# Clears and first loads of the next phase within the last batch, and a split of keys moved within its loop

## Time and profile before

| | us |
|---|---|
| three runs | 2462.93, 2463.0, 2460.99; median 2462.93 |
| profiled execution, own time | 2466.63 |
| its span, first to last instruction | 2464.5 |
| mean granted TensorE clock | 0.943 of full |
| busy: PE 2156.1, DVE 1533.1, ACT 1363.7, POOL 697.1 | shares 87%, 62%, 55%, 28% |

### The profile page before, as it was taken

One profiled execution on the slowest core, in us unless ns is written; L12 is line 12 of the kernel. 1 busy time (PEld: TensorE's weight loads), 2 busy tenths in 40 slices (PEclk: granted clock), 3 DMA queues, 4 the chain that ended last, 5 costly groups with the idle time before them and its releaser, 6 DMA issues. The chain is left out here.

```text
span 2464.5 us, 49127 instructions
## 1 busy us (share of the span) xinstructions
PE 2156.1 (87%) x15930; PEld 1268.1 (51%) x15930; DVE 1533.1 (62%) x3120; ACT 1363.7 (55%) x2226; POOL 697.1 (28%) x577
## 2 busy tenths in 40 slices
PE   3763899999999999999938999999998399999587
PEld 2331677777777777777724444444443144444132
DVE  2663788888888888888743434434432566666354
ACT  1441566666666666666724554454553166666464
POOL 1443544444444444444401122222123000000000
PEclk9885999999999999999968999999998699999799
DMA  5333111111111111111011122122211222222221
GB/s 179 104 114 91 33 36 33 33 33 33 33 33 33 33 33 33 33 32 32 20 31 60 65 94 67 56 90 68 94 69 34 73 91 90 89 89 69 90 90 35
DMA packets 156366, 151.01 MB, mean 61 GB/s; under 512 B 83656, under 2 KB 113874, under 8 KB 155026
## 3 DMA queue, kind: packets, MB, share of 16 engines
q1 hardware_dynamic: 150930, 148.11, 20.5%
q10 hardware_dynamic: 5376, 2.12, 0.3%
HBM read 96.08 MB, written 54.12 MB: 61 GB/s over the span
## 5 line engine op out<-in xcount | busy, mean ns | idle before, releaser
L1141 ACT ACTIVATE prob<-prob,neg_max_h 128x640 f32<-128x640 f32 x512 | 424.3, 829 | 329.4 <-DVE neg_max_h L1039 329.0
L1039 DVE CUSTOM_DVE_ANT_0 prob<-pair,pair_mask 128x640 f32<-128x640 f32 x512 | 418.9, 818 | 153.2 <-PE pair L956 153.0
L1102 POOL TENSOR_TENSOR a_full<-rot_c,rot_s 128x512 f32<-128x512 f32 x128 | 163.0, 1273 | 501.9 <-DVE rot_s L1026 501.9
L1622 PE MATMUL pair<-hid,down_w 128*128 128x512 f32 x640 | 295.6, 607 | 3.3 <-ACT hid L1548 3.3
L1046 DVE TENSOR_TENSOR prob<-prob 128x128 f32<-128x128 f32 x512 | 273.6, 534 | 0.5 <-ACT prob L1141 0.5
L1548 ACT ACTIVATE hid<-pair,up_b 128x512 f32<-128x512 f32 x320 | 198.6, 692 | 106.2 <-PE pair L1602 105.9
L912 PE MATMUL turn<-ident,prob 128*128 128x128 f32 x1024 | 250.4, 275 | 0.1
L912 PE MATMUL outsum<-ident,prob 128*128 128x128 f32 x1024 | 249.7, 275 | 0.5 <-ACT prob_t L1149 0.5
L1920 ACT ACTIVATE prob_h<-pair 128x512 f32<-128x512 f32 (+1 forms) x352 | 186.7, 561 | 102.7 <-PE pair L1820 98.5
L1875 DVE TENSOR_REDUCE row_max<-pair 128x1 f32<-128x384 f32 (+3 forms) x352 | 199.4, 634 | 32.6 <-PE pair L1795 31.9
L1622 PEld LDWEIGHTS pair<-hid,down_w 128*128 128x128 f32 x640 | 121.9, 193 | 150.9 <-issue 130.7
(11 more groups left out here) (270 smaller groups left out, 4324.1 us busy)
## 6 DMA issues: line engine op xcount, KB each, us to landing
o_d<-out_sb SPq DMA_DIRECT2D x64, 256.0 KB, 2.0
w_all<-w_d SPq DMA_DIRECT2D x8, 2048.0 KB, 10.8
vx_d<-vx SPq DMA_DIRECT2D x8, 1024.0 KB, 4.9
val_h<-vx_d SPq DMA_DIRECT2D x32, 256.0 KB
qs_d<-part_q SPq DMA_DIRECT2D x48, 128.0 KB
ks_d<-part_k SPq DMA_DIRECT2D x48, 128.0 KB
num<-o_d SPq DMA_DIRECT2D x24, 256.0 KB
den<-o_d SPq DMA_DIRECT2D x24, 256.0 KB
```

Of the source, the lines that this page charges most:

```text
L1039: nc.vector.tensor_tensor_reduce(prob[s % 4][:, :], pair[:, cols], pair_mask[:, cols], -1.0, 3.0e38, ALU.add, ALU.min, neg_max[par][:, s:s ...
L1102: nc.gpsimd.tensor_tensor(a_full[h % 2][:, :], rot_c[h % 2][:, :], rot_s[h % 2][:, :], ALU.add).then_inc(a_steps.sem, 1)
L1141: nc.scalar.activation(prob[s % 4][:, :], prob[s % 4][:, :], ACT.Exp, bias=neg_max[par][:, s:s + 1], scale=-1.0).then_inc(exp_done.sem, 1)
L1622: mm = nc.tensor.matmul(out_ap, down_w[:, EXPERTS[i], c, :], hid[i % 2][:, c, :], start=(c == 0 and i != 1), stop=(c == HC - 1 and i != 0))
```

## The change

1. `meet` is new: drain, count, wait, for some engines alone. PE, DVE, POOL and ACT meet between projection and layer-0 heads (`proj_met`, 4), PE, DVE and ACT between feed-forward and layer-1 heads (`ffn_met`, 3). SP is in neither. The three other barriers stay.
2. The clears of the layer-0 heads move into the projection's last batch: on DVE behind the rest of qu, on POOL between the last weight split and the last split of qv. Allocation is reordered so that the cleared tiles lie over nothing that is still in use, and three waits for stores are added within group 0 of the heads.
3. SP's first loads of the heads (`sp_first`) move into the last batch's stage 2, behind the store of the edge and ahead of the three stacks.
4. In every turn of the projection the keys' split stands right behind the edge product; keys are stored first of the three stacks.
5. In the feed-forward's `last`, DVE clears the layer-1 buffers behind the centre and writes the one-hot rows ahead of the queries' split; SP loads the first two groups ahead of the last stores; groups 2 and 3 are loaded by `h1_sp` behind the wait for all stores. ACT gets two waits for stores at its start.

```diff
+        def meet(eng, met, engines):
+            eng.drain().then_inc(met, 1)
+            eng.wait_ge(met, engines)
...
+        def clear_heads_v(v):
+            v.wait_ge(weight_parts.sem, weight_parts.at(2 * (B + NSH)))
+            for i in range(2):
+                nc.vector.memset(qs[i][:, :, :], 0.0).then_inc(heads_init, 1)
+                nc.vector.memset(ks[i][:, :, :], 0.0).then_inc(heads_init, 1)
+                nc.vector.memset(a_hi[i][:, :, S:AW], 0.0).then_inc(heads_init, 1)
+                nc.vector.memset(a_lo[i][:, :, S:AW], 0.0).then_inc(heads_init, 1)
+        def clear_heads_pool(g):
+            g.wait_ge(weight_parts.sem, weight_parts.at(2 * (B + NSH)))
...
             def stage2(b):
+                if isinstance(b, int) and b == B - 1:
+                    sp.wait_ge(v_stored.sem, v_stored.at(32 * (B - 1)))
...
                 sp.dma_start(one(ed_d, b), edge[:, :]).then_inc(edge_stored.sem, 16)
+                if isinstance(b, int) and b == B - 1:
+                    for stored in (qu_stored, qv_stored, k_stored):
+                        sp.wait_ge(stored.sem, stored.at(stack_dmas * (B - 1)))
+                    h0[5](sp)
+                sp.wait_ge(p2_dve.sem, p2_dve.at("k_3", b))
+                store_stack(sp, ks_d, b, part_k, k_stored.sem)
                 sp.wait_ge(p2_dve.sem, p2_dve.at("qu_3", b))
...
                 if project_of is not None:
                     edge_products(project_of)
+                    v.wait_ge(k_stored.sem, k_stored.at(stack_dmas * project_of))
+                    split(v, ve, kt, part_k, rest_k, p2_dve, "k", project_of)
...
                     rest_parts(qu, part_q, rest_q, "qu", project_of)
-                    v.wait_ge(k_stored.sem, k_stored.at(stack_dmas * project_of))
-                    split(v, ve, kt, part_k, rest_k, p2_dve, "k", project_of)
+                    if isinstance(project_of, int) and project_of == B - 1:
+                        clear_heads_v(v)
...
+            with g.Fori(0, B - 1) as b:
+                split_weights(b, b + NSH)
+                split_qv(b)
+            split_weights(B - 1, B - 1 + NSH)
+            clear_heads_pool(g)
+            split_qv(B - 1)
...
             def last(b):
                 store_x2(b)
                 load_mod1(b)
+                sp.wait_ge(v1_stored.sem, v1_stored.at(16 * b))
+                sp.wait_ge(q1_stored.sem, q1_stored.at(stack_dmas * b))
+                sp.wait_ge(k1_stored.sem, k1_stored.at(stack_dmas * b))
+                sp.wait_ge(h1_init, H1_INIT)
+                h1_load(sp, 0, 0)
+                h1_load(sp, 1, 1)
                 stores(b)
...
             def last(b):
                 ln1.center(v, "d", b, x2, f3_pe, f3_dve)
+                clear_h1(range(H1_BUFS))
                 adaln1(b)
                 bound_q(b)
                 bound_k(b)
+                one_hot_h1(v)
                 split_q(b)
...
             proj_sp(sp)
+            h0[0](sp)
             barrier(sp, 1)
-            h0[0](sp)
+            ffn_sp(sp)
+            h1_sp(sp)
             barrier(sp, 2)
...
             proj_v(v)
+            meet(v, proj_met, 4)
+            h0[2](v)
             barrier(v, 1)
-            h0[2](v)
+            ffn_v(v)
+            meet(v, ffn_met, 3)
+            h1_v(v)
             barrier(v, 2)
```

More of the change, by code:

```diff
@@ L327, in build @@
         a_lo = [sb(f"a_lo{i}", [P, GH, AW], BF16, heads_scope) for i in range(2)]
[L328 to L335, removed]
+        heads_init = sem("h0_heads_init")
+        N_INIT = 16
+        def clear_heads_v(v):
[7 more added lines that the diff above has]
+            g.wait_ge(weight_parts.sem, weight_parts.at(2 * (B + NSH)))
+            for i in range(2):
+                nc.gpsimd.memset(qvs[i][:, :, :], 0.0).then_inc(heads_init, 1)
+                nc.gpsimd.memset(wps[i][:, :, :], 0.0).then_inc(heads_init, 1)
+                nc.gpsimd.memset(val[i][:, :, :, DH:2 * DH], 1.0).then_inc(heads_init, 1)
+                nc.gpsimd.memset(val[i][:, :, :, 2 * DH:32], 0.0).then_inc(heads_init, 1)
         heads_scope.close()
@@ L1056, in dve_out @@
                 v.wait_ge(pv_done.sem, pv_done.at(NB * g + ib + 1))
+                if first(g) and ib == 0:
+                    v.wait_ge(qu_stored.sem, qu_stored.at(stack_dmas * B))
+                    v.wait_ge(k_stored.sem, k_stored.at(stack_dmas * B))
                 if ib == 0:
@@ L1148, in act_keep @@
                 act.wait_ge(pv_done.sem, pv_done.at(NB * g + ib - 1))
+                if first(g) and s == 0:
+                    act.wait_ge(xt_stored.sem, xt_stored.at(16 * B))
+                if first(g) and s == GH:
+                    act.wait_ge(qu_stored.sem, qu_stored.at(stack_dmas * B))
                 nc.scalar.copy(prob_t[ib % 2][:, h].rearrange("p b n -> p (b n)"), turns[s % 2][:, :]).then_inc(kept.sem, 1)
@@ L1758, in following, with h1_load @@
             return g + 1, (k + 1) % H1_BUFS, r + (k + 1) // H1_BUFS
+        def h1_load(sp, g, k):
+            load_q_stack(sp, q_h1[k], one(qs1_d, g), h1_loaded[k].sem)
+            load_k_stack(sp, k_h1[k], one(ks1_d, g), h1_loaded[k].sem)
+            sp.dma_start(val_h1[k][:, :, :, :].rearrange("p t h d -> p (t h d)"), one(vx1_d, g)).then_inc(h1_loaded[k].sem, 16)
         def h1_sp(sp):
[L1761 to L1764, removed]
             def group(g, k, r):
@@ L1770, in group @@
                     sp.wait_ge(h1_pv_done.sem, h1_pv_done.at(NB * (g + 1)))
[L1771 to L1775, removed]
+                    h1_load(sp, g + H1_BUFS, k)
+            for k in range(2, H1_BUFS):
+                h1_load(sp, k, k)
             with sp.Fori(0, NG // H1_BUFS - 1) as r:
@@ L1865, in h1_t, with clear_h1, one_hot_h1 @@
             values(NG - 1, H1_BUFS - 1, NB - 1)
+        def clear_h1(bufs):
+            for k in bufs:
+                nc.vector.memset(q_h1[k][:, :, :], 0.0).then_inc(h1_init, 1)
+                nc.vector.memset(k_h1[k][:, :, :], 0.0).then_inc(h1_init, 1)
+        def one_hot_h1(v):
+            nc.vector.memset(max_pad1[:, :, :], 0.0).then_inc(h1_init, 1)
+            v.wait_ge(h1_init, 1 + 2 * H1_BUFS)
+            for k in range(H1_BUFS):
+                for h in range(GH):
+                    nc.vector.tensor_copy(k_h1[k][KM:KM + GH, h, :],
+                                          identb[KM:KM + GH, KM + h:KM + h + 1].broadcast_to([GH, S])).then_inc(h1_init, 1)
         def h1_v(v):
@@ L2275, in _ @@
             proj_t(pe)
+            meet(pe, proj_met, 4)
+            h0[1](pe)
             barrier(pe, 1)
-            h0[1](pe)
+            ffn_t(pe)
+            meet(pe, ffn_met, 3)
+            h1_t(pe)
             barrier(pe, 2)
-            ffn_t(pe)
-            barrier(pe, 3)
-            h1_t(pe)
-            barrier(pe, 4)
             tail_t(pe)
@@ L2303, in _ @@
             proj_pool(g)
+            meet(g, proj_met, 4)
+            h0[3](g)
             barrier(g, 1)
-            h0[3](g)
+            ffn_pool(g)
             barrier(g, 2)
-            ffn_pool(g)
-            barrier(g, 3)
-            barrier(g, 4)
         @block.scalar
@@ L2315, in _ @@
             proj_a(act)
+            meet(act, proj_met, 4)
+            h0[4](act)
             barrier(act, 1)
-            h0[4](act)
+            ffn_a(act)
+            meet(act, ffn_met, 3)
+            h1_a(act)
             barrier(act, 2)
-            ffn_a(act)
-            barrier(act, 3)
-            h1_a(act)
-            barrier(act, 4)
             tail_a(act)
```

67 lines of the change are left out of this document (25 added, 42 removed).

## The result

The changed kernel takes 2409.14 us (median; 2403.72 to 2413.27), the kernel before 2462.97: a ratio of 0.9778 (95% interval 0.9765 to 0.979), 53.8 us faster. The forecast was 2409. Its profiled execution has a span of 2407.4 us, 57.1 under the span before.

| stretch | before | after | gained |
|---|---|---|---|
| first to last centre of the projection loop (six turns) | 120.8 | 94.8 | 26.0 |
| last centre to layer 0's first rotation on VectorE | 62.2 | 42.6 | 19.6 |
| first rotation to the last residual of the feed-forward | 1648.5 | 1648.7 | -0.2 |
| last residual to TensorE's first layer-1 matmul | 55.9 | 37.9 | 18.0 |
| that matmul to the tail's first load of the merge | 343.3 | 349.8 | -6.5 |

A forecast was written before the change was run, and what follows sets the result against it. The prediction took DVE to set the projection turn (20.31 us) and waiting chains to bound both edges; 15 + 23.2 + 15.9 = 54.1 us off the profiled 2466.6 gave 2412.5, median 3.7 lower: 2409, range 2392 to 2432.

The forecast's parts named there:

- Part 1: Projection loop: key split moved between centres and norms takes 2.70 us off 5.5 turns, 15 us gained (bounds 0 to 26).
- rival (d): Projection loop: the turn falls to 15.9 us since DVE meets POOL less; 65 us gained in all, 2398; chance 0.08.
- the upper bound, 26 us: Projection loop: with two of the last casts at the clean price, six turns lose 4.4 us each, 26 us.
- no cost, but no slack either: Projection loop: the wait for the key store, now in mid-turn, needs a turn of 16.4 to 17.5 us, just under 17.6.
- a sign of failure: Projection loop: forecast wrong if a DMA of the keys is named ahead of the split with a wait over 3 us.
- Part 2: Step from projection to layer-0 heads: first load at 212, PE starts at 219.0 instead of 242.21, 23.2 us gained (18 to 26).
- ACT has the first query part at 203.8 as before: First edge: ACT's first query part keeps its old time, so the clean 2.3 us query split ends at 206.3 to 208.4.
- Part 3: Step from layer-0 feed-forward to layer-1 heads: PE starts 18.4 us earlier, 2.5 us given back, net 15.9 us (8 to 22).
- PE stalls 2.5 us: Start of layer-1 heads: third group's load is ready 30.9 us after the first load, PE wants it at 28.4.
- (a): Projection loop: the key split gains nothing because it falls on POOL's work; 39.1 us gained in all, 2424; chance 0.12.
- (c): First edge: first loads do not come early, the edge gives 13 us; 44 us gained in all, 2419; chance 0.05.
- (b): Layer-1 heads: the third group's load comes 10 us late; 46.6 us gained in all, 2416; chance 0.10.

The follow-up runs named there:

- l: Changed kernel with a second set of the three key parts in the first loop, so VectorE's key split waits for no recent key store: 2409.89 us.
- i: Changed kernel with the third and fourth layer-1 loads put between the last value store and the last query and key stores: 2405.13 us.
- g: Changed kernel with layer 1's sixteen one-hot copies moved right behind the clears, ahead of the last batch's norm: 2396.08 us.
- m: Kernel before, with GpSimd's split of the other queries held back to the end of VectorE's key split, all batches but the last: 2465.54 us.
- e: Changed kernel with two extra GpSimd operations (1.04 us each) per batch, behind the wait for the landed store of the other queries: 2410.5 us.
- f: Changed kernel with two extra GpSimd operations (1.04 us each) per batch, ahead of the wait for the store of the other queries: 2409.48 us.
- h: Changed kernel with two sets of the other queries' parts, used in turn, so GpSimd's split waits for no recent store: 2419.71 us.

## Why the prediction came out

The total was right to a fraction of a us, the terms were not: 15, 23.2 and 15.9 us were forecast, 23.6, 20.1 and 10.2 measured in medians (26.0, 19.6 and 11.5 in the profiles). Errors of both signs cancelled, so that the total came out this close is luck.

**Part 1 was too small, and its mechanism only half right.** "So 2.70 us leave the end of the turn, 17.6 us remain" was the step that failed. The mean turn is 15.8 us: for the loop alone that is rival (d), which had 0.08. Only the first turn lost what was forecast for it, half of the 2.70 us (19.50 to 18.15). In the others the wait ahead of the norms went as forecast, but waits for the key store and for x took its place, and three quarters of the gain is busy time (19.6 of 26.0 us), because GpSimd's split moved off the affines and the query split. The prediction had this as the upper bound, 26 us, and counted two clean casts where all six operations of that stretch came out clean. The key store's wait, forecast as "no cost, but no slack either", is named in the trace (1.79 to 4.16 us), at one batch more than the 3 us that I had called a sign of failure: the store left 17.1 us behind its turn's centre (105.59 to 122.71), for 12.0 forecast, and landed in 8.3. Yet taking the wait out (l) gained nothing. The wait behind x's store was in no term of the sum.

**Part 2 was 3.6 us too large.** The first load left 34.7 us behind the last centre, for 30.8 forecast. The mis-sized terms are the clean prices of VectorE's two splits and "ACT has the first query part at 203.8 as before", 22.6 us behind that centre. The key split began 21.8 us behind it, within the forecast (20.1 to 22.2), but took 4.8 us for 2.7, and the query split 3.6 for 2.3. ScalarE's part was ready 26.6 us behind the centre: the query store is issued 16.1 us behind that centre for 15.3 and lands after 9.83 us for 6.7, with the keys' three stores ahead of it in the queue. Split and part were done at the same moment, so either alone would have held the query split. VectorE's clears cost what was forecast; GpSimd's took 7.3 us for 6.13, still under cover, but VectorE's slow casts ran beside them. First load to first matmul was 6.76 us for 6.98.

The page DMA: Bandwidth & Descriptors of the Trainium skill (Anatomy of one DMA), weighed in the prediction, gives its sum for a DMA that GpSimd issues; for this landing it would come to about 3 us as an estimate. The trace has 9.83 for stores that SP issues behind others in one queue, so the measurement decides against taking that figure here.

**Part 3 was right in its first half**: one-hot copies contended, 9.78 us where 5.5 + 4.3 was forecast (a price borrowed from the casts), first matmul 18.0 us earlier for 18.4. The give-back was mis-sized: "PE stalls 2.5 us" was 3.95, since the third load was ready 32.4 us after the first for 30.9, and what followed the stall made 6.5 of it. i shows that this is all of it, since without the stall the stretch is as before the change.

The SBUF page of the Trainium skill (SBUF — State Buffer, Who interferes with whom) says that copies can enter the modes that contend with GpSimd, and no row before showed whether these do. Here they do: the same sixteen copies, in the same program but for their place, took 9.78 us beside GpSimd's split and 5.50 without (g).

Rivals (a) and (c) didn't occur. (b) occurred in small: the loss at the third group is 6.5 us instead of 2.5.

What stays open: how much of the loop's gain needs the keys' place on VectorE and how much only their place in the store queue. No run moved the one without the other, and m's first turn speaks for a turn without waits alone. What sets the turn of about 16 us now is open too: x's store is the untested candidate, since no run takes that wait away. The 6 us that e and f add to the loop do not show in the total (2410.5 and 2409.48). In their profiles they come back in small pieces, mostly in stretches that they don't edit (e: 1.1 us at the first edge, 1.8 between it and the second, 3.0 in layer 1; f: 2.2 ahead of the first centre, 2.5 at the first edge, 2.3 behind the merge), and I can't say why.

## What to carry to other kernels

Where two engines slow each other down, read the duration of one and the same instruction in several places before counting instructions: here, when work was reordered, the difference between the clean and the contended price was a larger term (4.3 us in the turn shown) than the moved instructions themselves (2.70). The order of the stores in one queue decided here which wait ends late: with the keys first, the query store at the first edge took 3.1 us longer to land. A wait removed can be worth nothing if it was what kept two engines apart (h, l). Look for small preparations, like the one-hot copies, that can run while the neighbour engine idles.

## What the hardware showed that I had not expected

Not every VectorE instruction suffers beside GpSimd: the clears of 96 x 1024 words at the first edge ran beside GpSimd's split of the other queries (184.91 to 190.6) and took 0.91 us, as long as those of 128 x 1024 words at the second edge, where GpSimd idles. Casts of 128 x 512 went from 0.43 to mostly between 1.15 and 1.65, subtractions from 0.69 to between 1.41 and 1.64, and two float32 norms from 1.29 to 3.08. What GpSimd runs matters as well: beside its clears of 96 x 2048 at the first edge two casts took 1.56 and 1.65 us, but subtractions beside its clears of 96 x 1024 (at 179.78 and 183.39) stayed at 0.69.

A stall of 3.95 us on TensorE was followed by a granted clock of 0.72 over the 12.1 us that begin with it, and a matmul of 96 x 384 took 0.53 us in it for 0.33 ahead of it; with the stall taken out the clock there is 1.00. Taking the stall out gave back 6.2 us in i's profile (4.4 to 6.5 over all profiles without it), not 3.95; a stall of 2.38 us (h) left the clock at 1.00.
